# Edge columns before the splits, and expert results scattered by choice and token

## What is computed

```
xn  = layernorm(x)                                  # 1250 rows of 512
n   = xn + segment_sum(xn[src], dst)                # 40000 edges
g   = relu(n @ W1 + b1) @ W2 + b2 + xn              # 512 -> 1024 -> 512
a   = heads: relu(q k^T * 64**-0.5) v, 8 heads of 64, then W_out, + b_out
x2  = x + g + a
xt  = layernorm(x2)
p   = softmax(xt @ router_w.T + router_b)           # 16 experts, the best 2
out = x2 + sum over the 2 experts e of p_e * (gelu(xt @ w1_e.T + b1_e) @ w2_e.T + b2_e)
```

## Time and profile before

| what | value |
|---|---|
| three runs | 753.18, 752.69, 744.52 us |
| median | 752.69 us |
| the profiled execution's own time | 746.88 us |
| its span | 744.9 us |
| PE, PEld busy | 679.1 us (91%), 451.4 us (61%) |
| DVE, ACT, POOL busy | 461.1, 231.9, 152.8 us |
| share of the chain that ended last | PE 77%, DVE 6%, issue 5%, DMA 4%, POOL 4% |
| moved by DMA | 109.48 MB |

### The profile page before, as it was taken

The page is one execution under the profiler, slowest core; times in us unless marked ns, Lnnn a source line. Parts: engine busy times, 40 slices in busy tenths (PEclk is TensorE's granted clock), DMA queues, the critical chain, the costliest instruction groups (busy, mean ns, idle before and its releaser), DMA issues.

```text
span 744.9 us, 12323 instructions
## 1 busy us (share of the span) xinstructions
PE 679.1 (91%) x3840; PEld 451.4 (61%) x3841; DVE 461.1 (62%) x938; ACT 231.9 (31%) x472; POOL 152.8 (21%) x260
## 2 busy tenths in 40 slices
PE   4889999999999999999999999999997399999934
PEld 2545545455655655555554888989786277777601
DVE  5628753389888899797854995353544523433346
ACT  2312211223233233233334333332352144344300
POOL 6055110002124140332000700021302200000064
PEclk9999999999999999999999999999998599999955
DMA  9700000064361807273564900011209568854467
GB/s 294 205 0 0 1 3 1 29 255 154 146 236 64 299 2 284 98 259 117 186 230 156 409 9 0 1 44 44 85 4 403 193 234 283 264 192 127 141 196 231
DMA packets 48902, 109.48 MB, mean 147 GB/s; under 512 B 6842, under 2 KB 6858, under 8 KB 46384
## 3 DMA queue, kind: packets, MB, share of 16 engines
q1 hardware_dynamic: 44048, 88.97, 33.2%
q0 software_dynamic: 4768, 19.56, 8.5%
HBM read 47.35 MB, written 61.16 MB: 146 GB/s over the span
## 4 chain that ended last, share of the span: by engine, by line
PE 77%; DVE 6%; issue 5%; DMA 4%; POOL 4%; ACT 1%; SPq 1%; POOLq 0%; DVEq 0%; ACTq 0%
PE bank L1311 11%; PE bank L1294 10%; PE bank L1262 8%; PE bank L1228 7%; PE bank L1472 6%; PE bank L1406 6%; PE bank L1458 6%; PE bank L1349 6%; PE bank L1273 5%; PE bank L1192 4%; PE bank L1334 4%; POOL arena L626 2%; DMA arena<-in_x 2%; DVE arena L896 2%; PE bank L1433 2%
## 5 line engine op out<-in xcount | busy, mean ns | idle before, releaser
L896 DVE TENSOR_TENSOR arena<-iota,arena 125x384 f16<-125x384 f16 (+2 forms) x318 | 169.6, 593 | 23.2 <-POOLq L529 12.0
L703 ACT ACTIVATE arena<-bank 128x416 f32<-128x416 f32 (+1 forms) x120 | 62.2, 519 | 147.0 <-PE bank L1294 143.9
L1311 PE MATMUL bank<-arena 128*64 128x416 f32 (+1 forms) x480 | 97.2, 524 | 3.3 <-DVE arena L949 2.8
L949 DVE TENSOR_SCALAR arena<-bank 128x416 f32<-128x416 f32 (+1 forms) x120 | 67.4, 586 | 42.8 <-PE bank L1294 42.8
L527 POOL COPY arena<-arena 125x12 f32 (+1 forms) x80 | 34.9, 437 | 226.7 <-DVE arena L896 131.5
L1262 PE MATMUL bank<-arena 128*128 128x416 f32 (+1 forms) x192 | 75.1, 539 | 3.1 <-DMA arena<-in_wqkv 1.7
L1127 DVE COPY arena<-arena 128x1024 f32 x30 | 20.8, 694 | 63.5 <-issue 63.5
L1458 PEld LDWEIGHTS bank<-arena 128*128 128x128 f32 x448 | 53.0, 195 | 6.2 <-issue 6.2
L1192 PE MATMUL bank<-arena 125*128 125x160 f16 x471 | 51.4, 234 | 5.7 <-DVE arena L896 5.1
L1262 PEld LDWEIGHTS bank<-arena 128*128 128x128 f32 x192 | 36.4, 198 | 30.4 <-issue 28.5
L1192 PEld LDWEIGHTS bank<-arena 125*128 125x128 f16 x471 | 32.4, 98 | 36.6 <-issue 27.3
(11 more groups left out here) (231 smaller groups left out, 1145.0 us busy)
## 6 DMA issues: line engine op xcount, KB each, us to landing
slots<-arena SPq DMA_DIRECT2D x6, 5376.0 KB, 17.3
slots<-arena SPq DMA_DIRECT2D x2, 5120.0 KB, 16.6
arena<-in_ew SPq DMA_DIRECT2D x8, 1024.0 KB, 9.3
arena<-slots SPq DMA_DIRECT2D x32, 256.0 KB, 3.0
arena<-in_ew POOLq DMA_DIRECT2D x8, 1024.0 KB, 7.0
slots<-arena SPq DMA_DIRECT2D x28, 256.0 KB, 2.2
arena<-in_x SPq DMA_DIRECT2D x8, 512.0 KB, 7.4
arena<-in_gw SPq DMA_DIRECT2D x2, 2048.0 KB, 17.1
```

Source lines behind the costliest of these rows:

```text
L703: act.activation(probs[0:kt, s % NPB, 0, 0:n], bank[2 * (s % 2)][0:kt, 0:n], ACT.Relu).then_inc(p0_ready, 1)
L896: ins = dve.tensor_tensor(hot[:, :, c], iota16[0:CE, 0:width].unsqueeze(1).to_broadcast([CE, n, width]), window_cols[:, i % WBUF, of, k0:k ...
L949: dve.tensor_single_scalar(probs[0:kt, s % NPB, 1, 0:n], bank[2 * (s % 2) + 1][0:kt, 0:n], 0.0, op=ALU.max).then_inc(p1_ready, 1)
L1311: ins = pe.matmul(bank[AV][DH * a:DH * a + DH, 0:n], v_sb[0:kt, t, h * DH:h * DH + DH], probs[0:kt, s % NPB, a, 0:n], start=(t == 0), stop ...
```

## The change

1. In POOL's sorted list the two splits stand at turns 9.5 and 11.5 instead of 6.5 and 9.5, so the columns of windows 0 to 4 come ahead of them.
2. A row of `slots` (and of `x2n`, `xg` and the zeros) is 514 numbers instead of 512: behind the row lie a row id (YS + its number) and the reversed number of its first expert, which `pick` writes.
3. The tile loop's results go to a new DRAM buffer `ys` by indirect transfers on POOL, straight to row YS + token, or N further for the second choice; rows of unused slots go to a spill area. DVE works the addresses out in the loop from the two extra numbers (`row_facts`, `facts`, `dest`). SP no longer stores `y_sb`.
4. The reloads of `xg` in the loop move from SP to ACT, behind the copy of the transposes; both they and SP's second pair of loads also wait for DVE to have read the extra numbers. DVE waits at the head of each turn for the next rows. The late experts' loads and the counting move from POOL to SP.
5. After the loop `load_ys` reads `ys` with twelve plain transfers, six on SP and six on ACT, instead of 20 gathers. PE multiplies the second choice's rows by a diagonal matrix of gates (made ahead of the loop on DVE) on top of the biases in the bank, so DVE has two operations for a tile instead of three, and four more for the first four biases.

The other changed lines only move buffers by some bytes or declare semaphores.

```diff
+DW = D + 2
+YS = N + XS_ROWS
...
-    xs = nc.dram_tensor("slots", [XS_ROWS, D], f32, kind="Internal").ap()
+    xs = nc.dram_tensor("slots", [XS_ROWS, DW], f32, kind="Internal").ap()
+    ys = nc.dram_tensor("expert_rows", [YS + 2 * N, D], f32, kind="Internal").ap()
...
-        x2n = at(XN, [NT, D])
+        x2n = at(XN - 160, [NT, DW])
...
-        xg = at(S, [2, D])
-        xg_t = at(S + 4096, [2, KD, P])
-        hg_t = at(S + 8192, [2, KF, P])
-        y_sb = at(S + 10240, [2, D])
+        xg = at(S, [2, DW])
+        xg_t = at(S + 4128, [2, KD, P])
+        hg_t = at(S + 8224, [2, KF, P])
+        y_sb = at(S + 10272, [2, D])
...
+        gate_diag = at(5120, [NT, P])
+        tile_facts = at(13312, [MAXT, 2])
+        facts, row_facts, next_facts = (at(13824 + 64 * k, [2, 2]) for k in range(3))
+        dest, next_dest = at(14080, [2]).bitcast(i32), at(14144, [2]).bitcast(i32)
...
+        SUM_BANK = (0, 1, 0, 1, 6, 7, 2, 3, 6, 7)
...
+        def load_ys(engine, k):
+
+            engine.wait_ge(ys_done, 1)
+            of = ys[YS + k * N:YS + k * N + N, :]
+            of_v = of[0:(NT - 1) * P, :].rearrange("(t p) d -> p t d", p=P)
+            for i in range(LN_GROUPS):
+                last = min(2 * i + 2, NT - 1)
+                engine.dma_start(yg[:, k, 2 * i:last, :], of_v[:, 2 * i:last, :]).then_inc(yg_in[i], 16)
+            engine.dma_start(yg[0:LAST, k, NT - 1, :], of[(NT - 1) * P:N, :]).then_inc(yg_in[LN_GROUPS - 1], 16)
...
-                             zeros.unsqueeze(1).to_broadcast([P, len(fill) // P, D])).then_inc(zero_filled, 16)
+                             zeros.unsqueeze(1).to_broadcast([P, len(fill) // P, DW])).then_inc(zero_filled, 16)
...
+            def count_expert(e):
+                sp.wait_ge(ew_in[e], 16)
+                sp.sem_inc(w_ready, 1)
+
+            for e in range(6):
+                count_expert(e)
             sp.wait_ge(route_ready, 1)
             sp.wait_ge(scattered, 16 * 2 * NT)
             for a in range(2):
                 sp.dma_start(xg[:, a, :], rows_of(a)).then_inc(xg_in[a], 16)
+            sp.wait_ge(facts_read, 1)
             for a in range(2):
                 sp.wait_ge(xgt_ps[a], 1)
                 sp.dma_start(xg[:, a, :], rows_of(2 + a)).then_inc(xg_in[a], 16)
 
-            n = sp.value_load(npair[0:1, 0:1], min_val=1, max_val=(MAXT - 3) // 2)
-            with sp.Fori(0, n) as j:
-                for a in range(2):
-
-                    sp.wait_ge(xgt_ps[a], j + 2)
-                    sp.dma_start(xg[:, a, :], rows_of(2 * j + 4 + a)).then_inc(xg_in[a], 16)
-                for a in range(2):
-                    sp.wait_ge(y_saved[a], j + 2)
-                    sp.dma_start(rows_of(2 * j + a), y_sb[:, a, :]).then_inc(y_stored[a], 16)
-            for a in range(2):
-                sp.wait_ge(xg_in[a], 16 * (n + 2))
+            sp.wait_ge(xg_in[1], 32)
+            for e in (6, 7, 8, 11, 12, 13, 14, 15):
+                expert(e)
+                for landed in range(9 if e == 11 else e, e + 1):
+                    count_expert(landed)
+
+            load_ys(sp, 0)
             for t in range(NT):
                 sp.wait_ge(res_ready, t + 1)
                 sp.dma_start(out[t * P:t * P + rows(t), :], xr[0:rows(t), t, :]).then_inc(stored, 16)
...
+            ramp(row_ids[:, :], [[P, NT]], YS, 1)
+            ramp(spill[:, :], [[0, 1]], N, 1)
...
             for _, what, i in sorted([(start(max(w - 4, 0)), "cols", w) for w in range(NW)]
-                                     + [(min(6 * (p + 1), RAW) + 0.5, "split", p) for p in range(2)]
+                                     + [(max(FROM, RAW + 2 * p) + 0.5, "split", p) for p in range(2)]
                                      + [(summed[w // WPG], "spare", w) for w in range(0, NW, 2)]):
...
-            def count_expert(e):
-                pool.wait_ge(ew_in[e], 16)
-                pool.sem_inc(w_ready, 1)
-
-            for e in range(6):
-                count_expert(e)
-            pool.wait_ge(xg_in[1], 32)
-            late = [6, 7, 8, 11, 12, 13, 14, 15]
-            for e in late:
-                pool.dma_start(arena[:, expert_at(e):expert_at(e) + EW], ew[e]).then_inc(ew_in[e], 16)
-                for landed in range(9 if e == 11 else e, e + 1):
-                    count_expert(landed)
-
             pool.wait_ge(route_ready, 1)
             n = pool.value_load(npair[0:1, 0:1], min_val=1, max_val=(MAXT - 3) // 2)
-            for a in range(2):
-                pool.wait_ge(y_stored[a], 16 * n + 16)
-                pool.sem_inc(rows_stored, 1)
-            pool.wait_ge(rows_stored, 2)
-            for t in range(NT):
-                for k in range(2):
+            with pool.Fori(0, n) as j:
+                for a in range(2):
+                    pool.wait_ge(y_saved[a], j + 2)
+                    pool.sem_inc(rows_landed, 1)
                     pool.indirect_dma_start(
-                        out=yg[0:rows(t), k, t, :], out_offset=None, in_=xs,
-                        in_offset=bass.IndirectOffsetOnAxis(ap=slot[0:rows(t), k, t:t + 1], axis=0)
-                    ).then_inc(yg_in[t], 16)
+                        out=ys, out_offset=bass.IndirectOffsetOnAxis(ap=dest[:, a:a + 1], axis=0),
+                        in_=y_sb[:, a, :], in_offset=None).then_inc(y_stored[a], 16)
+                for a in range(2):
+                    pool.wait_ge(y_stored[a], 16 * j + 16)
+                    pool.sem_inc(y_free[a], 1)
+            pool.sem_inc(ys_done, 1)
...
+                    lies = act.value_load(tbase[0:1, bass.ds(2 * j + 4 + a, 1)], min_val=0, max_val=XS_ROWS - P)
+                    act.wait_ge(facts_read, j + 2)
+                    act.dma_start(xg[:, a, :], xs[bass.ds(lies, P), :]).then_inc(xg_in[a], 16)
+            for a in range(2):
+                act.wait_ge(xg_in[a], 16 * (n + 2))
+                act.sem_inc(rows_landed, 1)
             for t in FC_TILES[-1]:
                 act.wait_ge(gt_ps, t + 1)
                 act.activation(gates_t[:, t * P:(t + 1) * P], bank[t % 2][0:EXP, 0:P], copy).then_inc(gt_saved, 1)
+            load_ys(act, 1)
...
+                dve.tensor_copy(x2n[:, tt, D + 1], top)
+                dve.tensor_copy(x2n[:, tt, D], row_ids[:, tt])
...
             dve.sem_inc(route_ready, 1)
+            dve.tensor_scalar(tile_facts[:, :, 0], te[:, :], -1.0, float(EXP), ALU.mult, ALU.add)
+            dve.tensor_scalar(tile_facts[:, :, 1], tbase[:, :], spill[:, 0:1], None, ALU.add)
             weigh(len(FC_TILES) - 1)
 
             for a in range(2):
                 dve.sem_inc(y_saved[a], 1)
-                dve.sem_inc(y_stored[a], 16)
+                dve.sem_inc(y_free[a], 1)
...
                 take_w1(a, a)
+            for t in range(NT):
+                ins = dve.tensor_scalar(gate_diag[:, t, :], ident[:, :], gate[:, 1, t:t + 1], None, ALU.mult)
+            ins.then_inc(diag_ready, 1)
             n = dve.value_load(npair[0:1, 0:1], min_val=1, max_val=(MAXT - 3) // 2)
+            for a in range(2):
+                dve.wait_ge(xg_in[a], 16)
+            dve.tensor_copy(row_facts, xg[:, :, D:DW]).then_inc(facts_read, 1)
+            dve.wait_ge(facts_read, 1)
             with dve.Fori(0, n) as j:
+                for a in range(2):
+                    dve.wait_ge(xg_in[a], 16 * (j + 2))
+                dve.tensor_copy(next_facts, xg[:, :, D:DW]).then_inc(facts_read, 1)
                 for a in range(2):
                     dve.wait_ge(h_ps[a], j + 1)
                     take_w1(a, 2 * j + 2 + a)
+                dve.tensor_copy(facts, tile_facts[:, bass.ds(2 * j, 2), :]).then_inc(dest_steps, 1)
+                dve.wait_ge(dest_steps, 5 * j + 1)
+                dve.tensor_tensor(facts[:, :, 0], row_facts[:, :, 1], facts[:, :, 0], ALU.not_equal).then_inc(dest_steps, 1)
+                dve.wait_ge(dest_steps, 5 * j + 2)
+                dve.scalar_tensor_tensor(out=facts[:, :, 0], in0=facts[:, :, 0], scalar=float(N), in1=row_facts[:, :, 0],
+                                         op0=ALU.mult, op1=ALU.add).then_inc(dest_steps, 1)
+                dve.wait_ge(dest_steps, 5 * j + 3)
+                dve.tensor_tensor(next_dest, facts[:, :, 0], facts[:, :, 1], ALU.max).then_inc(dest_steps, 1)
+                dve.wait_ge(dest_steps, 5 * j + 4)
+                dve.tensor_copy(row_facts, next_facts).then_inc(dest_steps, 1)
+                dve.wait_ge(dest_steps, 5 * j + 5)
                 for a in range(2):
+                    dve.wait_ge(y_free[a], j + 1)
+                    dve.tensor_copy(dest[:, a:a + 1], next_dest[:, a:a + 1])
                     dve.wait_ge(y_ps[a], j + 1)
-                    dve.wait_ge(y_stored[a], 16 * j + 16)
                     dve.tensor_copy(y_sb[:, a, :], bank[6 + a][:, :]).then_inc(y_saved[a], 1)
 
+            for t in range(4):
+                dve.wait_ge(gb_ps, t + 1)
```

(37 more changed lines are left out.)

18 lines of the change are left out of this document (11 added, 7 removed).

## The result

The changed kernel takes 742.2 us, the median of 20 runs (738.8 to 749.9); the kernel before took 747.8 in its own 20 runs on the same chip (744.4 to 753.2). The ratio is 0.9935, with a 95% interval of 0.9913 to 0.9957: a gain of 0.65%, clear of the noise and inside two per cent. The profiled execution after took 744.22 us with a span of 742.5, against 746.88 and 744.9: 2.4 us less. So the sign was right and the size was not.

A forecast was written before the change was run, and what follows sets the result against it. PE was taken as the bound nearly everywhere, so only its waits or the last transfer could pay. Terms -6.0 + 0.3 + 2.2 + 0.5 - 6.2 = -9.2 us against the profiled 746.88 gave 738, range 731 to 753.

The forecast's parts named there:

- Step 1: Before turn 9: with columns ahead of the splits PE never stops and the clock holds, -6.0 us (-6.3 to -4.3).
- Rival D: Turn 9: PE still stops because something else, such as DVE's one-hots, comes at the same time; 744 us, chance 0.06.
- Step 2: Longer rows of `slots`: two more copies in each `pick`, fills still hidden, +0.3 us (0.2 to 0.8).
- Step 3: Entry of the tile loop: SP's second reload waits for DVE's first read and lands later, +2.2 us (0.8 to 3.5).
- PE's wait before the first turn's transposes 2.5 us instead of 0.34: Entry of the tile loop: the sign that would show the later landing of SP's second reload.
- Step 4: The 14-turn tile loop: added work on DVE, ACT and POOL fits, nearly every turn stays 7.88 us, +0.5 us (0 to 10).
- what is in hand, 4.9 us: Tile loop: time from ACT's issue of the second reload until PE needs that tile, 4.9 us.
- 5.4 at most: Tile loop: longest landing of a reload beside expert weights, 5.4 us, with 3.5 as the usual.
- rival C: Tile loop: the reload from ACT becomes the bound, 16 us lost, 754 us, slower than before; chance 0.13.
- Step 5: The end: plain loads, biases 4 to 7 at half clock, then DVE paces at 1.46 us a tile; -6.2 us.
- rival A: The end: the clock stays up through the biases and the loads bind; 734 us, chance 0.17.

## Why the prediction was wrong

**Step 1 failed**, at "PE never stops, and the clock has no reason to fall". The times in it were right: the edge columns did come early enough, and with the splits out of the way the stretch is 54.0 us, 6 below before. What failed is the cover given to the moved splits, "what is late next: the splits ... attention starts near 145". I asked who waits for them and when they are due, and not what else runs while they do. The 9.18 us in which DVE stood idle were not only the loss, they were also why the splits blocked nobody. The trace of before held the clue and I did not price it; its DVE and POOL at 62 us:

```profile
61.85 2.82 POOL L515 TENSOR_TENSOR k_lo<-arena,k_hi 128x1250 fp32r<-128x1250 f32 x1
62.25 2.97 DVE L929 TENSOR_TENSOR xn_lo<-arena,xn_hi 128x512 fp32r<-128x512 f32 x1
```

A subtraction of 0.69 us took 2.97 beside a single split. Moving pair 0's two casts and two subtractions into the stretch where DVE feeds PE, beside pair 1's, costs 1.4 + 1.05 + 3.4 us of PE's waiting, and 4.39 - 2.85 = 1.5 in the clock. The miss is 7.9 us (+1.9 for -6.0), more than the whole difference between the two spans and the forecast, 6.8.

**Rival D** named this outcome (PE stops all the same, for DVE's one-hots) at 744 with a chance of 0.06; it came true two to four turns later than it said. Its evidence against, DVE's idle time, was the idle time that the change takes away.

**Step 2** held: some 0.4 us for 0.3, and 3% on a fill where the prediction's estimate from the Trainium skill gave up to 25%. **Step 3** came out at 1.2 us instead of 2.2, but by luck. "PE's wait before the first turn's transposes 2.5 us instead of 0.34" did not come: PE waited for nothing there, and the time went into its first product, 5.63 us for 4.50, at half clock until about 601.0. That stretch of clock the prediction had put at nothing.

**Step 4** was mis-sized, +3.1 for +0.5. The count of what is in hand, 4.9 us, was if anything low: it was 5.5 and 5.3. The median landing of 3.9 us is near the 3.5 taken from the earlier trace rows too. What failed is "5.4 at most": the turns go by the longest landing, which was 7.1 us here, and 8.6 in the kernel before with late splits. The one trace that I had of the kernel before shows no turn that waits, and I took that for a bound. So the reload did become the loop's bound, as rival C has it, in two stretches of two turns, at 3 us and not 16; but the move to ACT is only in part its cause. PE had 5.8 us in hand where the old kernel was late (issued at 610.76, needed at 616.57), so the move took 0.3 to 0.5 us away. What makes single landings so long beside a weight load stays open; smaller loads did not end it.

**Step 5** was right in its order of events and 3 us too small. The loads and biases came as described, with biases 4 to 7 at half clock and DVE the bound from 726.6. The surplus: biases 2 and 3 still ran at the full clock (the fall came some 4.5 us after the last second product, where it had come 2.7 after it before), and DVE's pace was 1.39 us a tile for 1.46. So rival A was true for two biases.

The sum of the terms was -9.2 and the span moved by -2.4: +7.9 in step 1, +2.6 in step 4, -1.0 in step 3, -3.1 in step 5, +0.1 in step 2 and +0.3 by chance in the other stretches. With the splits placed late the kernel took 735.6 us, 2.4 below the forecast of 738, although the loop was late by as much; the larger gain at the end made up for that.

## What to carry to other kernels

An engine's idle time can be what makes its neighbour's work free. Before moving long POOL operations, list what DVE does in the new place; if those have two inputs in SBUF, move the POOL work elsewhere or cut it into pieces, which cost POOL two thirds more time and left DVE's one-hots at 1.07 us instead of up to 3.27. Size what a refill has in hand by its longest landing and not by the median, and over more than one profiled execution: one trace without a wait does not show that none comes.

## What the runs showed of the hardware

The clock fell to half while PE was busy without a gap, in products 16 rows deep, before (at about 708.4, PE busy 1.00 of 1.00 us). After, it held through 3.69 us of the same products, fell at about 717.2 at the end of a gap of 0.78 us, and then stayed at 0.50 while PE was busy without a gap (7.19 us for what had just taken 3.69). Alternating bias and diagonal products were left at 0.50 in one execution (2.00 us each, 713 to 717 us) and ran at the full clock in another of the same order (1.05 us each from 714.86 on). A reload of 257 KB beside loads of weights landed in 3.1 to 5.3 us at the median of a run, and single ones took 6.1 to 8.6, whether SP or ACT issued them. And runs of one program differ by several us from chance: a meeting of POOL and DVE that adds a microsecond, stretches of 20 us at a clock of 0.91, and such a landing.
